# Setup, first-image front and last-image back of a four-layer image kernel: laid out by the planner in parallel streams instead of one line of steps

## The reference

```
x = x + conv3x3(gn(x))                 # layer 0
x = x + mamba_block(gn(x))             # layer 1
x = x + coordinate_attention(gn(x))    # layer 2, with two small mambas over rows and columns
x = x + quantum_circuit(gn(x))         # layer 3, 4 qubits per pixel
```

```
dt = softplus(dtr @ dt_proj_w.T + dt_proj_b);  A = -exp(A_log)
h = exp(dt * A) * h + (dt * u) * B        # per token, per state
y = sum_n h * C                           # per token
```

## Time and profile before

| what | value |
|---|---|
| time, median of 3 runs | 14348.82 us (14336.92 to 14348.95) |
| the profiled execution: time / span of its core | 14312.51 us / 14310.7 us |
| mean granted TensorE clock | 0.930 |
| busy over the span: POOL / DVE / PE / ACT | 93% / 90% / 89% / 73% |
| from the start to the first unit | 141.6 us |
| from the last unit's sum to the end | 144.2 us |

### The profile page before, as it was taken

One profiled execution on the slowest core, in us unless ns is written; L12 is line 12 of the kernel. 1 busy time (PEld: TensorE's weight loads), 2 busy tenths in 40 slices (PEclk: granted clock), 3 DMA queues, 4 the chain that ended last, 5 costly groups with the idle time before them and its releaser, 6 DMA issues.

```text
span 14310.7 us, 203131 instructions
## 1 busy us (share of the span) xinstructions
PE 12685.4 (89%) x64796; PEld 8124.6 (57%) x64796; DVE 12945.1 (90%) x8813; ACT 10414.7 (73%) x14401; POOL 13340.7 (93%) x4106
## 2 busy tenths in 40 slices
PE   6899888899898998888998989988899989899886
PEld 3555555555555555555555555555555555555554
DVE  6999999999999999999999999999999999999985
ACT  5777777777777777777777777777777777777764
POOL 5999999999999999999999999999999999999985
PEclk8999999999999999999999999999999999999997
DMA  4655556555556555565555665556655655655553
GB/s 166 231 221 222 222 220 229 224 220 223 221 226 229 223 216 226 221 229 225 220 221 220 228 225 222 224 221 223 229 224 220 225 221 227 229 222 219 222 205 121
DMA packets 564038, 3134.39 MB, mean 219 GB/s; under 512 B 63826, under 2 KB 63834, under 8 KB 300642
## 3 DMA queue, kind: packets, MB, share of 16 engines
q1 hardware_dynamic: 562914, 3120.59, 58.0%
HBM read 3057.42 MB, written 46.14 MB: 217 GB/s over the span
## 4 chain that ended last, share of the span: by engine, by line
POOL 40%; issue 30%; PE 13%; DVE 11%; ACT 4%; DMA 1%; POOLq 0%; DVEq 0%; ACTq 0%; SPq 0%
POOL ring L965 25%; POOL ring L948 14%; PE work L1467 7%; DVE ring L1455 6%; DVE slot L1441 4%; PE y_acc L1482 3%; PE slot L1467 1%; PE y_acc L1467 1%; ACT L981 1%; ACT ring L1151 1%; DMA b_rows<-cb_rows_scratch 1%; POOL yz L915 1%; PE work L1482 1%; ACT u_conv L1020 0%; DVE du L1258 0%
## 5 line engine op out<-in xcount | busy, mean ns | idle before, releaser
L965 POOL TENSOR_TENSOR ring<-ring,c_rows 128x2048 f32<-128x2048 f32 x2048 | 9295.4, 4546 | 605.9 <-DVE ring L1455 603.2
L1455 DVE TENSOR_TENSOR_SCAN ring<-ring,slot 128x1024 f32<-128x1024 f32 x2432 | 5547.9, 2284 | 246.2 <-ACT ring L1151 10.7
L1482 PE MATMUL y_acc<-wk,ring 128*128 128x128 f32 x32768 | 4537.7, 287 | 461.9 <-POOL ring L965 300.7
L1482 PEld LDWEIGHTS y_acc<-wk,ring 128*128 128x128 f32 x32768 | 4016.9, 149 | 1551.0 <-issue 699.1
L948 POOL TENSOR_TENSOR ring<-du,b_rows 128x1024 f32<-128x1024 f32 x1664 | 3947.2, 2373 | 81.9 <-DVE du L1258 68.0
L1455 DVE TENSOR_TENSOR_SCAN ring<-slot,ring 128x1024 f32<-128x1024 f32 x1664 | 3783.9, 2274 | 202.1 <-POOL ring L948 139.3
L1151 ACT ACTIVATE ring<-dt,a_neg 128x1024 f32<-128x1024 f32 x2432 | 2721.3, 1138 | 106.4 <-PE y_acc L1482 74.4
L1441 DVE TENSOR_TENSOR slot<-du,slot 128x1024 f32<-128x1024 f32 x2176 | 2635.2, 1211 | 158.0 <-PE slot L1467 118.3
L1151 ACT ACTIVATE slot<-dt,a_neg 128x1024 f32<-128x1024 f32 x1664 | 1852.1, 1113 | 1084.1 <-DVE ring L1455 1076.7
L1467 PE MATMUL work<-h_new,fused 128*128 128x512 f32 x4096 | 1975.9, 612 | 72.8 <-ACT b_t L1063 24.2
L1467 PE MATMUL slot<-stack,sel 96*128 96x512 bf16 x4352 | 1431.5, 413 | 495.4 <-DVE ring L1455 455.3
(11 more groups left out here) (182 smaller groups left out, 11343.5 us busy)
## 6 DMA issues: line engine op xcount, KB each, us to landing
c_rows<-cb_rows_scratch SPq DMA_DIRECT2D x2048, 1024.0 KB, 4.7
b_rows<-cb_rows_scratch SPq DMA_DIRECT2D x1664, 512.0 KB, 5.4
x_next<-in_x SPq DMA_DIRECT2D x32, 512.0 KB, 6.5
x_new_scratch<-x_next SPq DMA_DIRECT2D x32, 512.0 KB, 6.7
h_old<-h_new SPq DMA_DIRECT2D x32, 512.0 KB, 2.9
x_old<-x_new_scratch SPq DMA_DIRECT2D x32, 512.0 KB, 5.6
out<-x_old SPq DMA_DIRECT2D x32, 512.0 KB, 2.9
cb_rows_scratch<-stack SPq DMA_DIRECT2D x128, 96.0 KB
```

Of the source, the lines that this page charges most:

```text
L965: pool.tensor_tensor(pair, pair, c_rows[:, k % CB_BUFS, :, :], ALU.mult).then_inc(prod_ready, 1)
L1455: dve.tensor_tensor_scan(slot, a, b, 0.0, MUL, ADD).then_inc(scan_done, 1)
L1482: ins = pe.matmul(chunk(out_t, j), chunk(x, j), kc("ident"), is_transpose=True, start=start and j % (BANK // P) == 0, stop=stop, skip_grou ...
```

## The change

`in_turn` is gone. `begin_plan()` hands `lay()` eight streams: front and operands of image 0 as one, the first time steps as another, and six of setup (`zero`, weights, decays, batch-norm scales, mixes, circuit). Only the true dependences are added between them: the front waits for `zero`, `nin` for `bn1`'s shift, `conv_in` for the last `fuse`, the time steps for `a_neg2` and `diag`, and `m1` for the step `h1`. `finish_plan()` hands it two: mix and back, and the four `decays2`. PSUM steps of setup now use a bank of the two (`w`) instead of the tile `work`. ACT and PE wait for the weights themselves, since DVE is no longer ahead of them all. The sync engine waits for `kron 2 2` before its four small circuit DMAs and, before it loads rows over the weights, for the last user of each. Some costs are added to the planner's table; none is of a step that the plans of the images contain. The instructions of all 32 images' unit loops stand in the same order as before.

```
-def setup():
-    s = [(("zero",), "G"), (("small_bf16",), "D")]
...
+def set_up():
+    weights = [step(("small_bf16",), "D")] + [step(("fuse", f, k), "D") for f in range(2) for k in range(TAPS)]
+    weights += [step(("diag", h), "D") for h in range(HALVES)]
+    decays = [step(("a_exp",), "A"), step(("a_exp2",), "A"), step(("a_neg",), "D"), step(("a_neg2",), "D")]
...
+    circuit += [step(("m1",), "P", "m1", [("h1", 1)]), step(("m1_copy",), "D", "m1"), step(("q_neg",), "D"),
+                step(("tt",), "P", "tt"), step(("tt_copy",), "D", "tt"),
...
+    return [[step(("zero",), "G")], weights, decays, scales, mixes, circuit]
...
+def held_back(steps, *after):
+    (name, e, bank, more), *rest = steps
+    return [step(name, e, bank, (*more, *after))] + rest
+
+def best_plan(streams, kind, paces):
+    plan, length = min((lay(streams, kind, pace) for pace in paces), key=lambda x: x[1])
...
+def begin_plan():
+    f, o, t = front(), operands(0), timestep(0, 0)
+    h1, silu = ([x[0] for x in f].index(("nin", 0)), 0)
+    f = held_back(f[:h1], ("zero",)) + held_back(f[h1:], ("bn_shift", "bn1"))
+    o = held_back(o, ("fuse", 1, TAPS - 1))
+    t = held_back(t, ("a_neg2",), ("diag", HALVES - 1))
+    return best_plan([f + o, t] + set_up(), "begin", PACES)
+
+def finish_plan():
+    decays = [x for m in range(2) for h in range(HALVES) for x in decays2(m, h)]
+    return best_plan([mix() + back(), decays], "finish", PACES)
...
-    before, finish = in_turn(lead + lead2 + begin), in_turn(mix() + back(False))
+    before, finish = begin_plan(), finish_plan()
...
-            sp.wait_ge(*done(NONE, before_n[before[lead2_at - 1][1]]))
+            sp.wait_ge(*done(NONE, before_n[("kron", 2, 2)]))
...
-            sp.wait_ge(*done(NONE, before_n[before[begin_at - 1][1]]))
+            for last_use in (("postw_mask", CH - 1), ("mixw_copy", 1, HALVES - 1), ("fuse", 1, TAPS - 1)):
+                sp.wait_ge(*done(NONE, before_n[last_use]))
...
+            act.wait_ge(weights_in, 16 * 7)
...
+            pe.wait_ge(weights_in, 16 * 7)
```

More of the change, by code:

```diff
@@ L250, in back @@
     return s
-def setup():
-    s = [(("zero",), "G"), (("small_bf16",), "D")]
-    s += [(("fuse", f, k), "D") for f in range(2) for k in range(TAPS)]
-    s += [(("diag", h), "D") for h in range(HALVES)]
-    s += [(("a_exp",), "A"), (("a_exp2",), "A"), (("a_neg",), "D"), (("a_neg2",), "D")]
+def set_up():
+    weights = [step(("small_bf16",), "D")] + [step(("fuse", f, k), "D") for f in range(2) for k in range(TAPS)]
+    weights += [step(("diag", h), "D") for h in range(HALVES)]
+    decays = [step(("a_exp",), "A"), step(("a_exp2",), "A"), step(("a_neg",), "D"), step(("a_neg2",), "D")]
+    scales = []
@@ L262, in setup @@
     for f in range(2):
         for h in range(HALVES):
[L264 to L278, removed]
+            b = ("mixw", f, h)
@@ new lines, in set_up @@
+            mixes += [step(("mixw", f, h), "P", b), step(("mixw_copy", f, h), "D", b)]
+    circuit = [step((k,), "D") for k in ("q_sum", "q_diff", "q_quarter", "q_up", "q_down", "q_frac")]
+    circuit += [step(("q_sin",), "A")]
+    circuit += [step(("gate", k), "D") for k in range(8)] + [step(("gate_negs",), "D")]
+    circuit += [step(("kron", n, i), "D") for n in range(3) for i in range(3)]
+    circuit += [step(("m1",), "P", "m1", [("h1", 1)]), step(("m1_copy",), "D", "m1"), step(("q_neg",), "D"),
+                step(("tt",), "P", "tt"), step(("tt_copy",), "D", "tt"),
+                step(("blocks",), "P", "blocks"), step(("blocks_mask", 0), "D", "blocks"), step(("blocks_mask", 1), "D", "blocks"),
+                step(("postw",), "P", "postw")] + [step(("postw_mask", j), "D", "postw") for j in range(CH)]
@@ L440, in lay @@
 def lay(streams, kind, pace, soon_within=SOON, shifts=()):
-    programs = unit_programs(kind)
+    programs = unit_programs(kind) if kind in ("first", "mid", "last") else dict.fromkeys("PADG", [])
     by = {("result", 1): 2 * OUT_AT - 8, ("dt_u", 0, 0, 1): UNITS - 4, ("part", 0, 2, 1): UNITS - 2}
@@ L466, in lay @@
             want[x[0]] += .5 * more
-    free, at = dict(dict.fromkeys("PADG", 0.) if kind == "first" else LAG), dict.fromkeys("PADG", 0)
+    free, at = dict(LAG if kind in ("mid", "last") else dict.fromkeys("PADG", 0.)), dict.fromkeys("PADG", 0)
     end = {("sum", -1): free["P"]}
@@ L534, in lay @@
     return plan, max(free[e] - LAG[e] for e in LAG)
+def held_back(steps, *after):
[3 more added lines that the diff above has]
+    plan, length = min((lay(streams, kind, pace) for pace in paces), key=lambda x: x[1])
+    if plan is None:
+        raise ValueError("the steps do not fit")
+    return plan
+def begin_plan():
[8 more added lines that the diff above has]
+    return best_plan([mix() + back(), decays], "finish", PACES)
 def image_plan(first, last):
     kind = "first" if first else "last" if last else "mid"
-    def held_back(steps, *after):
-        (name, e, bank, more), *rest = steps
-        return [step(name, e, bank, (*more, *after))] + rest
     def pass_end(d, h):
@@ L591, in image_plan @@
     streams += [takes, zs]
[L592 to L596, removed]
+    return lay(streams, kind, PACE, WITHIN, SHIFTS)[0] if kind == "mid" else best_plan(streams, kind, PACES)
 def four_layers(nc, images, x_in, keep, once, small, dtw, conv_wt, preb_row, qw, out):
@@ L1206, in step @@
                     _, f, h = name
-                    ins = dve.tensor_scalar(mixw[:, f, h, :], work[:, 0:P], 0.25, None, MUL)
+                    ins = dve.tensor_scalar(mixw[:, f, h, :], w[:, 0:P], 0.25, None, MUL)
                 elif k == "q_sum":
@@ L1238, in step @@
                 elif k == "m1_copy":
-                    ins = dve.tensor_copy(m1, work[0:AMPS, 0:4 * AMPS])
+                    ins = dve.tensor_copy(m1, w[0:AMPS, 0:4 * AMPS])
                 elif k == "q_neg":
@@ L1242, in step @@
                 elif k == "tt_copy":
-                    ins = dve.tensor_copy(ttc, work[0:AMPS, 0:2 * AMPS])
+                    ins = dve.tensor_copy(ttc, w[0:AMPS, 0:2 * AMPS])
                 elif k == "blocks_mask":
```

38 lines of the change are left out of this document (16 added, 22 removed).

## The result

The changed kernel takes 14266.4 us (median of 5 runs, 14244.4 to 14279.4), the kernel before beside it 14348.8 us (14332.3 to 14378.2, 5 runs): ratio 0.994, 95% interval 0.9925 to 0.9955. The profiled execution takes 14274.0 us, its span 14272.2.

The account below looks back on a forecast made before the run. Middle near engine limits, both ends chains of one engine at a time; gains of 41.1 us at the start and 7.7 at the finish, 48.8 off 14348.8, give 14300.0 us, range 14270 to 14332.

Parts of the forecast that it names:

- Setup leaves the chain: Start: image 0's first moment no longer waits for setup and begins near 14.3 instead of 52.16; gain 37.9 us.
- The first norm queues behind VectorE's setup: Start: `group_eps`, wanted at 17.6, waits for VectorE's setup work until 18.4; loss 0.9 us (0 to 2).
- Three `mixw` among the convolutions: Start, from `conv0` to `conv_in`: three setup matmuls on PE delay the convolutions; loss 1.0 us (0.6 to 2.4).
- The circuit inside `conv_in`: Start, from `conv_in` to `xproj`: circuit steps issued between its steps cost 2.0 us (1 to 4); `postw` costs nothing.
- Two streams from `xproj` on: Start, from `xproj` to first unit: second-half operands lie beside the first time step; 30.6 becomes 23.5 us, gain 7.1.
- The rivals of the front: Start: inserted waits keep TensorE at 1.2 GHz, costing 25.3 us more, time 14325; chance 0.07.
- B's rows: Start, row loads before the first unit: expected hidden; as a rival, late rows cost 3 us, 14303, chance 0.04.
- The finish: End of kernel: each of four small-mamba passes hides 1.9 us from `dta2` to `spread2`; gain 7.7 us (6 to 8).
- the same 48.8 off 14348.8 gives 14300.0: Whole kernel: the total gain at both ends, taken from the profiled execution, is subtracted unchanged from the timed median.
- The rival that spoke of the images: Middle images: their time depends on when they start, 1 us each costing 30; chance 0.07 of over 20 us.

Follow-up runs that it names:

- `one_front`: The changed kernel with front, operands and first time step of image 0 as one stream again (seven streams, not eight); 14257.9 us, run once.
- `after_late`: The changed kernel with 42 extra ScalarE copies of the first image ahead of its first moment; 14282.4 us, ratio 0.9956 to the kernel before.
- the fillers: Unused memsets ahead of VectorE's first instruction: one in the kernel before, ratio 0.9969; one in the changed kernel, 0.9963; two there, 0.9939.
- `again_before`: The kernel before, unchanged, profiled and timed once more; 14353.9 us, ratio 1.0003.

## Why the prediction was right, and where it failed

**Setup leaves the chain.** Right: 52.16 - 14.43 = 37.7 us, forecast 37.9.

**The first norm queues behind VectorE's setup.** The row is there, smaller: from moment to `conv0` 6.09 us against 5.78, a loss of 0.3 where I took 0.9. `group_eps` started at 17.94; 18.4 was forecast.

**Three `mixw` among the convolutions.** From `conv0` to `conv_in` 33.94 us against 32.93: 1.0, as forecast. The copy at 40.41 that waited 5.31 us for PE shows that PE was late and not VectorE, as argued.

**The circuit inside `conv_in`.** 22.10 us against 20.11: 2.0, as forecast, 0.70 of it in the row at 62.73. `postw` cost nothing.

**Two streams from `xproj` on.** 21.43 us against 30.59: gain 9.2, forecast 7.1. The term was undersized by what it left out: the first `dt_proj` starts 1.8 us behind the end of the first `xproj` instead of 11.4, and takes 1.12 us where the old one took 2.07; and the five row copies hid better than I allowed. Against `one_front` the second stream is worth 8.7 us in this stretch.

**The rivals of the front.** TensorE was not kept slow: 1.00 in 20.5 to 42.9 (by the page; its first four records still took 3.78 us, some 0.95 each, the old block's first three 2.93) and 0.88 in `conv_in`, with the 16 records of its second half in the same 7.14 us as before. In 42.90:54.50, where PE was busy 4.54 of 11.60 us, the clock is 0.65, and within the first `conv_in` steps it is back: two records take 2.05 us at 54.46, eight take 3.70 us at 62.73. By the Trainium skill, "TensorE: Matmul & The Clock Gate", section "What's actually happening", activity releases the throttle; the trace agrees with these numbers. B's rows were in time: their load is issued at 89.51, 2.0 us behind the step that ends at 87.53, and no input waits for a DMA.

**The finish.** 14209.21 - 14201.51 = 7.70 us a pass where it was 9.64: about 7.7 saved in four, as forecast. Some 1.0 us more came off other steps of the finish.

**The sum and the step that failed.** The ends give 52.3 us, the forecast 48.8, so of the miss 3.5 us lie in my terms. The other 30 lie in the step "the same 48.8 off 14348.8 gives 14300.0": it takes for granted that the middle of the changed kernel lasts as long as that of the kernel before, since its instructions are the same. They are, and it doesn't. The rival that spoke of the images asked whether they answer to when they start; `after_late` shows that the gain stays without the earlier start, though whether the start's time has a part of its own is open. What the fillers show them to answer to is where VectorE's code lies. The new start has one VectorE record fewer, and a pause of 0.36 us that stood ten times on the path went under a scan. I gave the images 0.07 for the bad side and said that the good side was as likely, but let it widen the range by 14 us only, from 14284 to 14270, where 30 were needed: the earlier trace rows, with 6 us from one image to the next, were the warning, and the price of 30 us for 1 us an image stood in the text.

**The profiled execution as a base.** The kernel before was profiled in an execution whose 30 images took 13115.9 us; the five other traces with the pause exposed took 13143.0 to 13157.0. That is why it lay 36.3 us under the median, and why two profiles laid side by side give 38.5 us and the medians 82.

How the 0.36 us become 3 us is shown in part. Exposed ten times, they are 3.6 us by themselves. The rest arises where the windows above show it, in stretches in which matmuls wait for small ScalarE and VectorE steps: a shift of some tenths of a microsecond ahead of them goes with another clock (0.81 and 0.84) for the same matmuls. `after_late` shows that a shift of all images together does not take the gain away, and the DVE fillers that a delay repeated in every turn goes with a loss of it. Why the repeated delay should mostly lengthen the turn and not as often shorten it stays open. What the pause is, I can't show either. That the visible ones stand about 128 records or a multiple apart, and that the one at the scan moves with the program, points to the supply of instructions, and the page's part 3 lists two queues named "instruction", with 560 and 564 packets in the kernel before. The packed trace of `again_before` adds a hint: most packets of the second of them are of 8 KB, and if one takes every 128th VectorE record from the 71st of a turn on, such a packet starts between 0.3 us before and 0.7 us behind it in 25% of the cases; for every 128th record from an arbitrary one it is 3% on average. No run tied a packet to a pause.

## What to carry to other kernels

Ends of a kernel in which one engine works at a time can be read step by step from the timeline, and laying independent chains beside each other pays there what the rows say, to a few us. A tightly balanced loop is another matter: its time can change by 0.2 to 0.3% because the code ahead of it grew or shrank by one instruction on one engine, so a gain or loss of that size is to be claimed for an edit only after the same kernel has run with a filler instruction or two. And a forecast made from one profiled execution should carry the spread of the unchanged part in its range, in both directions.

## What the runs showed of the hardware

- VectorE pauses for 0.35 to 0.38 us between two records at places of its program that stay the same from turn to turn, 127 to 129 records or a multiple of 128 apart (455, 583, 966, 1350 of a turn in `again_before`). On the path it shows as idle time of 0.47 us where 0.12 is usual. It is free under a long instruction (the scan of 2.29 us in the changed kernel), and where a wait behind it takes it up (record 72 in `after_late`, 0.37 us made up within 15 us).
- At the branch that closes the loop the next record comes 1.97 to 1.98 us later on VectorE, 4.95 to 5.18 us on ScalarE and 0.34 to 0.40 us on GpSimd, each of the nine times that it is taken, in all fourteen traces.
- A delay of 0.34 us in a turn of 1320 us came out as 8.2 us at its end, 6.3 of them in two stretches of some 67 us in which the same matmuls ran at a granted clock of 0.81 and 0.82 instead of 0.84; VectorE and ScalarE were busy as long there as in the other run, within 0.3 us.
